# Layer 1's feed-forward one slot later in a hand-written slot table of a two-layer transformer kernel, with its spike comparisons re-placed

## What is computed

```python
x = x + jnp.tanh(g_xattn[1]) * _L1_xattn_ref(_layernorm(x), ctx, ctx, wq, bq, wk, bk, wv, bv, wo, bo)
x = x + jnp.tanh(g_ffn[1])   * _L1_ffn_ref(_layernorm(x), W_fc, W_proj)

# _L1_xattn_ref, per head:  probs = softmax(q k^T / 4); out = probs v; then out @ wo + bo
# _L1_ffn_ref:
h = jnp.square(jax.nn.relu(jnp.einsum('bsd,fd->bsf', x, W_fc)))     # 1024 hidden
y = jnp.einsum('bsf,df->bsd', h, W_proj)
def step(mem, _):
    reset = spike_fn(mem - 1.0)
    mem_new = 0.9 * mem + y - reset
    return (mem_new, spike_fn(mem_new - 1.0))
_, spks = jax.lax.scan(step, zeros, None, length=5)
return jnp.sum(spks, axis=0) / 5
```

## Time and profile before

| | |
|---|---|
| Time, median of 3 runs | 1348.85 us (1346.96 to 1358.17) |
| The profiled execution | 1347.56 us, span of its instructions 1344.9 us |
| PE busy | 1022.2 us, 76% |
| DVE busy | 855.5 us, 64% |
| ACT busy | 641.0 us, 48% |
| POOL busy | 621.5 us, 46% |
| POOL gathers `x_tok` (L1888) | 168 times, 274.5 us, 14% of the chain that ended last |
| Row maxima (L1778) | 256 times, 164.1 us, idle before them 68.6 us, of it 65.6 us for the maxima on PE |

### The profile page before, as it was taken

One profiled execution on the slowest core, in us unless ns is written; L12 is line 12 of the kernel. 1 busy time (PEld: TensorE's weight loads), 2 busy tenths in 40 slices (PEclk: granted clock), 3 DMA queues, 4 the chain that ended last, 5 costly groups with the idle time before them and its releaser, 6 DMA issues.

```text
span 1344.9 us, 26475 instructions
## 1 busy us (share of the span) xinstructions
PE 1022.2 (76%) x8597; PEld 703.1 (52%) x8597; DVE 855.5 (64%) x1982; ACT 641.0 (48%) x1128; POOL 621.5 (46%) x844
## 2 busy tenths in 40 slices
PE   4997889887508898888322656888888888899886
PEld 2665656555308888888210223555555554565564
DVE  3775666756625666866532654767677677787654
ACT  2443234334406676676210343666655556665662
POOL 0157788778861212111467768382746556000000
PEclk9999999998758999999656667998898989899997
DMA  8343464323338888887637565454545545111110
GB/s 302 131 169 143 179 218 151 115 111 113 120 127 245 278 280 271 270 276 229 224 67 128 82 123 92 108 89 101 106 104 112 97 100 97 50 52 48 42 34 16
DMA packets 127731, 188.25 MB, mean 140 GB/s; under 512 B 21872, under 2 KB 101360, under 8 KB 127088
## 3 DMA queue, kind: packets, MB, share of 16 engines
q1 hardware_dynamic: 93040, 133.06, 30.6%
q0 software_dynamic: 34560, 53.50, 18.0%
HBM read 98.15 MB, written 75.24 MB: 129 GB/s over the span
## 4 chain that ended last, share of the span: by engine, by line
POOL 16%; PE 16%; DVE 8%; issue 7%; DMA 2%; ACT 2%; DVEq 1%; POOLq 0%; ACTq 0%
POOL x_tok L1888 14%; PE bank L347 8%; PE bank L1590 3%; DVE row_max L1778 3%; PE bank L1546 2%; DMA x_tok<-ys,y_row 2%; POOL prob L1918 1%; DVEq L1843 1%; PE bank L1527 1%; DVE spikes L1844 1%; PE bank L1504 1%; ACT hid L1668 1%; DVE v_one L1764 1%; POOL rstd L1896 1%; POOL mixed L1918 1%
## 5 line engine op out<-in xcount | busy, mean ns | idle before, releaser
L1888 POOL DMA_INDIRECT x_tok<-ys,y_row x168 | 274.5, 1634 | 53.5 <-issue 48.6
L1778 DVE TENSOR_REDUCE row_max<-bank 128x2 f32<-128x512 f32 x256 | 164.1, 683 | 68.6 <-PE bank L1504 65.6
L1644 ACT ACTIVATE prob<-bank 128x512 f32<-128x512 f32 x256 | 137.5, 589 | 87.1 <-PE bank L1527 83.4
L1006 POOL DMA_INDIRECT xs<-w_hi,slot_row x144 | 146.5, 1017 | 56.4 <-DVE slot_row L893 33.9
L1274 POOL COPY row_share<-row_tile 128x1 f32 x224 | 45.2, 248 | 193.9 <-DMA row_tile<-xs 182.7
L1900 POOL TENSOR_TENSOR rstd_f<-var_eps_f,minus_half 128x2 f32<-128x2 f32 x16 | 14.3, 894 | 218.4 <-DVE var_eps_f L1707 218.4
L1504 PE MATMUL bank<-k_stack,q_stack 48*128 48x256 f16 x512 | 54.8, 294 | 72.3 <-DVE row_max L1778 66.4
L347 PE MATMUL bank<-xf_hi,w_hi 128*128 128x256 f16 x256 | 76.4, 298 | 35.9 <-DVE xf_lo L1827 28.4
L1113 PE MATMUL bank<-ident,row_tile 128*128 128x128 f16 x896 | 62.1, 225 | 44.8 <-issue 24.1
L347 PE MATMUL bank<-xt_tile,w_routed 128*128 128x128 f16 x1344 | 91.5, 228 | 0.0
L1160 ACT ACTIVATE xt_tile<-bank 128x1024 f16<-128x1024 f16 x56 | 57.4, 1025 | 61.5 <-PE bank L1113 60.6
(11 more groups left out here) (218 smaller groups left out, 2655.5 us busy)
## 6 DMA issues: line engine op xcount, KB each, us to landing
row_tile<-xs SPq DMA_DIRECT2D x224, 144.0 KB, 3.0
ys<-y_tile SPq DMA_DIRECT2D x56, 512.0 KB, 3.9
w_routed<-in_weights_r SPq DMA_DIRECT2D x4, 2048.0 KB, 10.4
inverse<-den_mid SPq DMA_DIRECT2D x64, 128.0 KB
xs<-zeros SPq DMA_DIRECT2D x32, 144.0 KB, 3.1
ctx_t<-in_ctx SPq DMA_DIRECT2D x8, 512.0 KB, 3.7
ct_mid<-ct SPq DMA_DIRECT2D x8, 512.0 KB, 2.6
ct<-ct_mid SPq DMA_DIRECT2D x8, 512.0 KB, 4.5
```

The lines of the kernel that those rows point to most:

```text
L1006: nc.gpsimd.indirect_dma_start(xs[:, :], bass.IndirectOffsetOnAxis(slot_row[p][:, tt, k:k + 1], axis=0), x_whole[g % 3][:, tt, :], None) \
L1644: nc.scalar.activation(prob[:, h % NPR, :, :], seconds.bank((n, h))[:, :], ACT.Exp, scale=float(HD) ** -0.5).then_inc(seconds.reader((n, h ...
L1778: V.tensor_reduce(row_max[n % PAIR][:, :, m, j], firsts.bank((n, 2 * j + m))[:, :].rearrange("p (q k) -> p q k", q=2), AX_X, ALU.max).then ...
L1888: nc.gpsimd.indirect_dma_start(x_tok[g % NXT][:, tt, :], None, ys[:, :], bass.IndirectOffsetOnAxis(y_row[:, g * TT + tt, k:k + 1], axis=0) ...
```

## The change

Two lines of numbers. `UP_AT` moves from `WO_AT + 8` to `WO_AT + 9`; since `COUNT_AT`, `FIRED_AT` and `LAST` are worked out from it, all ups, downs, their ACT and DVE steps and the last addition stand one slot later for every sequence, while the transposes (`F_AT`), `high_f` and `low_f` stay. The five comparisons get new offsets from `COUNT_AT`, so their slots become, modulo 16, 12, 13, 14, 0, 2 (before 10, 12, 14, 0, 1).

```diff
-            F_AT, UP_AT = WO_AT + 6, WO_AT + 8
+            F_AT, UP_AT = WO_AT + 6, WO_AT + 9
             DOWN_LAG = 4
             COUNT_AT = UP_AT + 2 * (UPS - 1) + DOWN_LAG + 1
-            COUNTS = (0, 1.5, 3.5, 5.5, 6.2)
+            COUNTS = (.5, 1.2, 2.5, 4.5, 6.5)
```

## The result

| | kernel before | kernel after |
|---|---|---|
| median of 20 runs each, us | 1347.53 (1338.68 to 1358.17) | 1360.19 (1350.71 to 1363.9) |
| the profiled execution, us (its span) | 1347.56 (1344.9) | 1357.19 (1355.4) |
| ratio after : before, 95% interval | | 1.0081 [1.0062, 1.0099] |

The changed kernel is slower by 0.81%, or 10.9 us [8.4, 13.3]. The first part of the page of the kernel after answers to the earlier trace rows: busy us, share of the span, instructions.

A forecast was written before the change was run, and what follows sets the result against it. No engine is full (PE busiest, 76%), so waits decide, with stretches bound by DVE, PE and POOL's gathers in turn. Terms -3.2 + 10.4 + 2.6 - 2.8 = +7.0 us on 1347.56 gave 1354.6 us, range 1342 to 1366.

The forecast's parts named there:

- rival A: Whole kernel: the sum of the terms holds, net +3 to +11 us, 1350 to 1359; chance 0.48.
- The largest term, between rm0 and rm1: On DVE, `hid_lo` comes late behind count4 and divide; PE waits at d0: 1.3 us in eight uncovered halves, +10.4 us.
- s4 ahead of up0: On PE, s4 fits into the wait for `xf_lo` before up0: a gain of 0.4 us times 8, -3.2 us.
- wo ahead of d2: On PE, nothing while PE is full; in the drain it shortens the chain of sequences 13 to 15, -4.2 us.
- count0 behind `xn_f`: On DVE, count0 leaves the wait for POOL and delays `low_f`: 0.65 us in four turns, +2.6 us.
- The drain: Last sequences, no maxima left: wo gains 4.2 us, count0 between `xn_f` and `low_f` costs 1.4; together -2.8 us.
- The cover in the gather halves: Halves of sequences 1, 3, 5, 7 last as long as POOL's gathers, hiding losses under 3.45 us.
- B: PE's 1.2 GHz stretch lengthens with the new wait before d0: 8 x 1.25 = 10 us more, 1364.6; chance 0.16.
- R1: Rival set for the experiments, on PE: the clock follows the new wait and makes most of the loss; no chance given.
- D: up0 starts at 2.4 GHz, winning up to 2.5 us per uncovered half: 1339.6, or 1324 to 1335; chance 0.10.
- C: The 1.3 us delay dies in PE's wait before m7, or no wait at d0 appears: -3.4 us, 1344; chance 0.16.
- E: Uncovered halves too end at POOL, so only sequences 9 to 11 pay, 3 x 0.9 us: 1350; chance 0.10.

The follow-up runs named there:

- den_early: Kernel after with the reciprocal of the denominators and its store moved earlier: ratio to the kernel before 1.0043 [1.0019, 1.0067], 1350.79 us.
- hidback: Kernel after with all `low_hid` one slot earlier, so the first `hid_lo` stands ahead of divide: ratio to the kernel before 1.0006 [0.9975, 1.0037], 1353.96 us.
- ups_only: Kernel after with the comparisons and all `low_hid` at their old places: ratio to the kernel before 0.9985 [0.9955, 1.0014], 1343.83 us.
- counts_only: Kernel before with only the comparisons moved to their new places: ratio to the kernel before 0.9971 [0.9938, 1.0004], 1351.23 us.
- ups_x: Kernel after with comparisons and `low_hid` at old places, transposes of x one slot later: ratio to the kernel before 0.9956 [0.9928, 0.9984], 1343.65 us.
- hid_late: Kernel before with only all `low_hid` moved one slot later: ratio to the kernel before 1.0258 [1.0210, 1.0307], 1380.38 us.
- ups_x_den: Kernel after, comparisons and `low_hid` at old places, transposes of x one slot later, reciprocal and store earlier: ratio to before 0.9904 [0.9867, 0.9941], 1335.67 us.
- c4back: Kernel after with count4 put back beside count3, ahead of rm0: ratio to the kernel before 1.0061 [1.0030, 1.0091], 1362.35 us.
- x_later: Kernel after with the transposes of x one slot later: ratio to the kernel before 1.0080 [1.0049, 1.0111], 1360.50 us.

## Why the prediction was right

The forecast was 1354.6 us, +7.0 against the profiled 1347.56, within 1% by the sum of rival A. Measured were +10.9 us [8.4, 13.3], and +6.9 on the second chip (1.0051 of 1354.8; 3 to 11). Sign, mechanism and place were right; the terms were not all so, and that the sum still came within 4 us is in part luck, as errors of both signs are in it.

**The largest term, between rm0 and rm1: right in kind, too small.** I had `hid_lo` start 4.3 us after rm0 and m2 at 7.4, a loss of 1.3 us, eight times. Where no DMA came between it was nearly so: 4.35 and 7.59 us for sequence 10, 4.36 and 7.59 for sequence 11. In the other six halves m2 came 7.15, 8.17, 9.17, 7.68, 11.02 and 8.56 us after rm0 (sequences 0, 2, 4, 6, 8, 9). The distance over that of the kernel before sums to 17.1 us in the eight halves, in place of 10.4. The step that failed is "divide 1.13", taken from a place where its input had landed. The change puts divide ahead of `hid_lo` and 0.4 to 0.5 us nearer to rm0, and I had not asked when the inverse arrives. In these eight halves divide waited 0.99, 0.49, 1.49 and 2.18 us for it (sequences 0, 2, 4, 8), 5.2 of the 6.7 us that were missing; another 1.2 is the clock, below. den_early removes those waits and brings m2 of sequences 2, 4 and 8 to 7.65, 7.59 and 7.94 us. Sequence 9 lost its 1.84 us with no wait at d0: there the wait for x's bank (2.30 us) came first. The total did not rise by as much: 6.7 us more in this term would make the sum 13.7, just over the upper end of the measured interval, 13.3.

**Where the rest stayed.** From rm0 of sequence 0 to rm0 of sequence 11, the trace of the kernel after took 392.9 us and that of the kernel before 385.6, so 7.2 more. Counted from each rm0 to the next, the uncovered halves grew by 15.5 us, nearly all of it between rm0 and m2, and the covered ones shrank by 8.3. Of these 8.3, 6.7 lie between `low_f` of a covered half and the next rm0, that is, at up0 of sequences 2, 4, 6 and 8. In the trace on which the prediction was made PE ran there at 0.50 to 0.59, in the kernel after at 1.00 for 2, 4 and 8. That need not be an effect of the change: in the second execution of the kernel before all four ran at 1.00, while `power_x` to `power_f` took 30.4 to 30.6 us there, where the first trace has mostly 29.55. The first four microseconds of up0 of sequence 4 in the kernel before, its second execution and the kernel after (columns as in the earlier trace rows):

```profile
983.15:987.15 4.00, 4.00 (x32) 2.00 (x32) 2.44 (x4) 1.86 (x4) 3.35 (x3) 0.59 0.76 161
984.17:988.17 4.00, 4.00 (x44) 2.40 (x45) 2.89 (x5) 2.43 (x5) 3.39 (x3) 1.00 0.75 137
984.71:988.71 4.00, 4.00 (x45) 2.57 (x46) 2.52 (x5) 2.43 (x5) 3.39 (x3) 1.00 0.74 166
```

So two single traces must not be subtracted as if the change were all that differs. The part before layer 1 shows it too: its first maxima (L1504) start at 711.1 and 716.2 us in the two executions of the kernel before, at 716.5 and 722.2 in those of the kernel after. From there to the end it is 633.8 and 634.3 us before, 638.9 and 647.7 after, and 634.1 in hidback.

**s4 ahead of up0, -3.2 us: seen in the rows, not in the total.** The wait for `xf_lo` did shrink, from 1.95 to 1.75 us in the mean (21.5 us and 19.3, 11 times each), as forecast in kind (0.3). Where PE runs at full clock, `low_f` to the next rm0 fell from 4.38 us (both executions of the kernel before) to 4.06, so 0.32 us where I took 0.4; where it runs at 1.2 GHz no gain shows (6.53 and 6.58 us for sequence 1). ups_only, which has this term and wo ahead of d2 but not count0's new place, gained 0.15% [-0.14, 0.45], that is 2 us where -3.2 and -4.2 make 7.4, more than its interval allows (6).

**count0 behind `xn_f`, +2.6 us: wrong.** counts_only, which has it, was not slower. The row by which I priced it behaved nearly as said: `xn_f` to `low_f` took 7.73 us (1049.26 to 1056.99) in place of 7.26, forecast 7.9. From the DVE timeline of the kernel after, the first and the last of that stretch:

```profile
1049.26 0.79 DVE L1821 TENSOR_SCALAR xn_f<-x_tok,moments_f,rstd_f 128x256 f32<-128x256 f32 x2 [0.98 <-POOL rstd_f L1900]
...
1056.99 0.69 DVE L1827 SCALAR_TENSOR_TENSOR xf_lo<-bank,xf_hi 128x512 f16<-128x512 f32 x1
```

A swap of one instruction from one side of a wait to the other was priced as a loss, and what count0 freed ahead of `xn_f` (PE and ACT had their rm5 and `qk_hi` earlier) was not. That this is the reason is argued, not shown.

**The drain, -2.8 us: not resolved.** From the `low_f` of sequence 12 to the end it took 93.9 us in place of 95.1, but 97.5 in the second execution of the kernel after and 99.6 in that of the kernel before. The last sequences came no closer together: from `low_f` to `low_f` it was 24.6, 23.1 and 24.2 us, before 24.7, 23.1 and 21.5. With the comparisons and `hid_lo` at their old places the drain is short, 90.0 us in ups_only and in ups_x, so wo ahead of d2 may be worth its 4.2 us; one execution each does not settle it. The last sequence's `xn_f` to `low_f` grew by 0.94 us (3.15 in place of 2.21; forecast 0.7), and d3 of the sequence before it met a wait that I had not counted, because its `hid_lo` stands behind the moments there:

```profile
1329.69 0.28 PE L1590 MATMUL bank<-w_hi,hid_hi 128*128 128x256 f16 x1 [1.76 <-DVE hid_lo L1833]
```

**The cover in the gather halves: right, but thinner than thought.** `power_x` to `power_f` took 29.1 us (before 29.55), and `xn_f` still waited for POOL in four turns, 2.20, 2.21, 0.98 and 2.36 us. hid_late showed what it costs when that cover is used up.

**The rivals.** B, the clock, was right in one place. Windows of the kernel after, around d0 of sequence 6, just after up0, and behind d0 of sequence 8 (columns as in the earlier trace rows):

```profile
1064.50:1080.00 15.50, 13.85 (x123) 8.96 (x120) 11.55 (x20) 10.38 (x19) 2.60 (x1) 1.00 0.28 63
1019.50:1024.60 5.10, 5.10 (x38) 2.61 (x38) 2.37 (x5) 2.29 (x5) 4.31 (x4) 0.60 0.56 119
1142.00:1148.00 6.00, 6.00 (x43) 2.51 (x44) 4.07 (x6) 2.07 (x5) 0.00 (x0) 0.72 0.14 48
```

At sequence 6 PE lost 1.65 of 15.5 us, and PEclk is 1.00. So it is behind the waits of 0.74 to 2.78 us in six of the seven places from 849 to 1243 us at which PE waits for `hid_lo`. Behind the wait of 3.48 us it is 0.72: for some three of the six microseconds PE ran at 1.2 GHz. mix2 took 1.94 us there and not 1.07, and m2 came 4.39 us behind `hid_lo` in place of 3.23, so 1.2 us went that way, where B asked 1.25 in each of eight. In the second execution of the kernel after PEclk was 0.72 behind two of the seven waits, of 3.10 and 3.50 us, and m2 came 1.1 and 1.5 us later there. The clock followed only where the DMA had made the wait long. Against R1 as the main cause stands its size, 1.2 and 2.5 us in the two traces. D named up0 at full clock as its sign. The second row shows a place of a covered sequence where PE still works partly at 1.2 GHz (PEclk 0.60, before 0.51); at up0 of sequences 2, 4 and 8 the sign did appear, but the second execution of the kernel before has it too, so the change is not shown to be its cause, and D's gain is not shown either. C fell by the 12.3 us at L1590. Of E one half was so: parts of the loss are hidden, by POOL and by the wait for x's bank, but the turns with gathers paid: four of them, from `power_x` to `power_x`, took 294.3 and 297.5 us in the two executions of the kernel after, 290.3 and 288.1 in those of the kernel before.

**The rule of the Trainium skill** that I had set against the change, in "TensorE: Matmul & The Clock Gate", section "Step-by-step: what each phase is for", that PE is the only engine that reorders, so that VectorE works through its queue in order, is borne out by 1135.91 to 1141.16: `hid_lo` did not pass a divide that stood 2.18 us on a DMA. "Perfetto Trace Analysis", section "Optimization Strategy", advises to make what the most contended engine waits for start sooner or end faster. ups_x_den, at 0.9904, does that for `hid_lo` as against the kernel after, and for the inverse, for which DVE and not PE waits; for the bank of x it moves the waiting instruction later instead. PE's wait for `xf_lo`, to which by that advice one would have gone first, was left (16.8 us) and no run here worked on it.

## What to carry to other kernels

When a change shifts a step in a strict queue, look first at which producer the critical engine waits for next, and at everything that now stands ahead of it; sum their durations, and for each ask also when its own inputs land, DMAs above all. A wait that vanishes from the list may only have stood ahead of another one at the same place (the bank of x and `hid_lo`): taking it away with `hid_lo` still late gained nothing. Two executions of one kernel can differ in a single trace by more than the change does, so take a second trace of the kernel before as well. And the steps around a moved one have to be placed anew: the ups one slot later did not pay, but with `hid_lo`, the transposes of x and the reciprocal placed to suit the kernel was 0.96% [0.59, 1.33] faster than before. No run has those placements with the ups at their old slot, so what the slot itself gives there is not shown.

## What the runs showed of the hardware that I had not expected

Whether a wait of PE in full work costs clock does not go by its length alone in these traces. Behind 2.78 us (kernel after), 3.25 us (c4back) and 3.28 us (x_later) PEclk stayed at 1.00 for the next six microseconds; behind 2.33 us (hid_late, four times) and 2.10 (x_later) it was 0.72 on average. The same program at the same place, up0 of sequence 4, ran at 0.59 in one execution and at 1.00 in another. Which of the two comes was not found out. And the inverse of the denominators, which goes to memory and back, needed 3.42 and 3.75 us for its two transfers in the chain above. That is longer than any other step of the stretch between rm0 and m2, and no row of DVE's order shows it.
